# Two attention layers on one core: keys put into class order by ScalarE as they leave PSUM, queries read at a stride of four by the score products

## What is computed

```python
pos = jnp.arange(seq_len)
seg = pos // 64
local = seg[None, :] == seg[:, None]
diff = jnp.abs(pos[None, :] - pos[:, None])
dil = (diff > 0) & (diff % 4 == 0) & (diff <= 4 * 64)
mask = jnp.where(local | dil, 0.0, -jnp.inf)
scores = jnp.einsum('bqhd,bkhd->bhqk', q, k) * scaling + mask
out = jnp.einsum('bhqk,bkhd->bqhd', softmax(scores), v)
```

## Time and profile before

| what | value |
|---|---|
| time, median of three runs | 470.29 us (467.96, 470.29, 470.34) |
| span of the profiled execution | 468.2 us |
| TensorE matmuls busy | 443.3 us, 95% |
| VectorE busy | 394.1 us, 84% |
| ScalarE busy | 333.0 us, 71% |
| GpSimd busy | 296.5 us, 63% |
| granted TensorE clock | 0.998 |

### The profile page before, as it was taken

How to read it: one execution, slowest core, us unless ns; L and a number is a source line. 1 busy time by engine, 2 the same in 40 slices (tenths; PEclk the granted TensorE clock), 3 DMA queues, 4 the chain that set the end, 5 groups by cost and what they waited for, 6 DMA issues and landing times.

```text
span 468.2 us, 17264 instructions
## 1 busy us (share of the span) xinstructions
PE 443.3 (95%) x6440; PEld 348.8 (74%) x6440; DVE 394.1 (84%) x1344; ACT 333.0 (71%) x975; POOL 296.5 (63%) x491
## 2 busy tenths in 40 slices
PE   7999699999999999999999899998987989999996
PEld 5687588888888888888787678887744757558775
DVE  5888598997988899799797697996899989998775
ACT  3678668778768777877786678695566579987533
POOL 4222576687576768667865587665669897674322
PEclk9999999999999999999999999999999999999999
DMA  6477952356345335445455564464000000000003
GB/s 224 175 254 201 276 122 53 75 115 123 75 84 110 74 74 109 81 78 109 86 116 122 110 135 90 77 123 91 1 1 0 0 2 0 2 0 2 1 0 91
DMA packets 136098, 40.53 MB, mean 87 GB/s; under 512 B 104976, under 2 KB 131024, under 8 KB 136016
## 3 DMA queue, kind: packets, MB, share of 16 engines
q1 hardware_dynamic: 135440, 38.38, 35.9%
q10 hardware_dynamic: 576, 1.05, 0.6%
HBM read 29.44 MB, written 9.96 MB: 84 GB/s over the span
## 4 chain that ended last, share of the span: by engine, by line
PE 59%; POOL 9%; DMA 8%; DVE 8%; ACT 7%; SPq 4%; issue 3%; ACTq 0%; POOLq 0%; DVEq 0%
PE psum L464 10%; PE psum L422 10%; PE psum L484 5%; PE psum L1186 5%; PE psum L498 5%; PE psum L495 4%; PE psum L510 4%; PE psum L403 4%; DMA st<-w_rows_dram 3%; DMA w_rows_dram<-st 3%; PE psum L1181 3%; ACT pband L569 3%; PE psum L405 2%; PE psum L404 2%; POOL area L1827 2%
## 5 line engine op out<-in xcount | busy, mean ns | idle before, releaser
L948 POOL TENSOR_SCALAR pband<-pband,fac 128x192 f32<-128x192 f32 x256 | 103.9, 424 | 84.8 <-DVE fac L771 84.7
L569 ACT ACTIVATE pband<-pband,st 128x192 f32<-128x192 f32 x256 | 113.2, 448 | 0.9 <-DVE st L719 0.9
L719 DVE CUSTOM_DVE_ANT_0 pband<-psum,band_mask 128x192 f32<-128x192 f32 x256 | 76.0, 353 | 0.1
L422 PE MATMUL psum<-keys,q_class 64*64 64x192 f32 (+2 forms) x1536 | 66.3, 274 | 0.0
L464 PEld LDWEIGHTS psum<-ident,pband 128*128 128x128 f32 x384 | 45.3, 141 | 25.5 <-issue 17.8
L464 PE MATMUL psum<-ident,pband 128*128 128x128 f32 x384 | 53.1, 273 | 6.1 <-DVE arena L836 3.1
L422 PEld LDWEIGHTS psum<-keys,q_class 64*64 64x64 f32 x1536 | 57.7, 133 | 1.4 <-issue 1.4
L569 ACT ACTIVATION_READ_ACCUMULATOR pband<-pband,st 128x1 f32 x256 | 49.5, 193 | 0.0
L938 POOL COPY q_class<-q_rows 128x512 f32<-128x512 f32 x32 | 36.4, 1137 | 14.0 <-ACT q_rows L609 14.0
L930 POOL COPY keys<-k_rows 128x512 f32<-128x512 f32 x32 | 36.2, 1131 | 14.3 <-issue 7.2
L780 DVE COPY pt<-psum 128x512 f32<-128x512 f32 x64 | 43.6, 682 | 0.4
(11 more groups left out here) (213 smaller groups left out, 1086.4 us busy)
## 6 DMA issues: line engine op xcount, KB each, us to landing
v_rows_dram<-arena SPq DMA_DIRECT2D x32, 256.0 KB, 4.6
v_both<-v_rows_dram SPq DMA_DIRECT2D x32, 256.0 KB, 3.9
v_seg<-v_rows_dram SPq DMA_DIRECT2D x64, 128.0 KB, 3.8
v_side<-v_rows_dram SPq DMA_DIRECT2D x96, 64.0 KB, 2.6
w_rows_dram<-st SPq DMA_DIRECT2D x64, 8.0 KB, 3.0
st<-w_rows_dram SPq DMA_DIRECT2D x64, 8.0 KB, 2.5
arena<-_attn_hidden_states_dram SPq DMA_DIRECT2D x4, 256.0 KB, 3.9
out_dram<-x SPq DMA_DIRECT2D x4, 256.0 KB, 2.5
```

What stands on the lines that cost most here:

```text
L422: return pe.matmul(bank[2 * r + head][rows, at:at + y.shape[1]], x, y, start=True, stop=True, skip_group_check=True)
L569: act.activation(x, x, ACT.Exp, bias=mine[:, head:head + 1], scale=-1.0, accum_out=mine[:, 2 + head:3 + head]).then_inc(s_exp, 1)
L719: dve.tensor_tensor_reduce(pband[:, G % P_SLOTS, c, head, :], bank[2 * r + head][:, at:at + BAND], band_mask[:, (0, 1, 1, 2)[w], SEG * (1 ...
L948: pool.tensor_scalar(x, x, fac[:, F % 2, 1, c, head:head + 1], 1.0, ALU.mult, ALU.mult).then_inc(s_scaled, 1)
```

## The change

ScalarE's `take_keys` writes straight into `keys`: it reads the bank at a stride of four, and writes four runs of 128. `k_rows`, `q_class`, `keys_by_class` and `queries_by_class` are gone, and with them the semaphores `s_kclass` and `s_qclass`. The band products read the stationary queries out of `q_rows` at a stride of four numbers (16 bytes). The segment products stream their 64 keys out of `keys`: sixteen positions by four classes, where the class runs fastest, and a class lies 640 numbers (2560 bytes) from the next. A `zero_pads` function only wraps three lines that were there.

```diff
-        k_rows = sb("k_rows", [P, ROW_SLOTS, WT])
         q_rows = sb("q_rows", [P, ROW_SLOTS, WT])
-        q_class = sb("q_class", [P, ROW_SLOTS, DIL, P])
...
                 if r == 0:
-                    pe.wait_ge(s_qclass, G + 1)
-                    pe.wait_ge(s_kclass, G + 1)
-                    if w < NW - 1:
-                        pe.wait_ge(s_kclass, G + 2)
+                    pe.wait_ge(s_query, G + 1)
+                    pe.wait_ge(s_key, G + (2 if w < NW - 1 else 1))
...
-                    x0, x1 = (q_class[DH * head:DH * (head + 1), G % ROW_SLOTS, c, :] for head in range(2))
+                    x0, x1 = (q_rows[DH * head:DH * (head + 1), G % ROW_SLOTS, :].rearrange("p (x c) -> p c x", c=DIL)[:, c, :]
+                              for head in range(2))
...
                             cols = slice(P * a + SEG * half, P * a + SEG * (half + 1))
+                            first_x = PAD + P * w + CLASS_SEG * (2 * a + half)
                             last = product(head, rows, at, q_rows[dims, G % ROW_SLOTS, cols],
-                                           k_rows[dims, G % ROW_SLOTS, cols])
+                                           keys[dims, p % 2, :, first_x:first_x + CLASS_SEG].rearrange("q c x -> q x c"))
...
                 act.wait_ge(s_proj[1], t + 1)
-                wait(act, s_score, 2 * (t - ROW_SLOTS + 1))
-                wait(act, s_kclass, t - ROW_SLOTS + 1)
-                act.copy(k_rows[:, t % ROW_SLOTS, :], shared_bank[:, :]).then_inc(s_key, 1)
+                p, w = divmod(t, NW)
+                if t == 0:
+                    act.wait_ge(s_const, CONST)
+                wait(act, s_score, 2 * NW * (p - 1))
+                act.copy(keys[:, p % 2, :, PAD + P * w:PAD + P * (w + 1)],
+                         shared_bank[:, :].rearrange("p (x c) -> p c x", c=DIL)).then_inc(s_key, 1)
...
                 wait(act, s_score, 2 * (t - ROW_SLOTS + 1))
-                wait(act, s_qclass, t - ROW_SLOTS + 1)
                 act.copy(q_rows[:, t % ROW_SLOTS, :], shared_bank[:, :]).then_inc(s_query, 1)
...
             for t in range(FIRST_STEP, DRAIN):
                 scale_band(t - 5, 1)
-                keys_by_class(t)
+                
                 scale_seg(t - 5)
                 scale_band(t - 4, 0)
-                queries_by_class(t - 1)
+                
```

More of the change, by code:

```diff
@@ L12 @@
+import math
 from contextlib import ExitStack
@@ L189, in attention @@
     s_proj, s_key, s_query = [sem("s_proj_q"), sem("s_proj_k")], sem("s_key"), sem("s_query")
-    s_kclass, s_qclass = sem("s_kclass"), sem("s_qclass")
     s_score, s_max, s_segmax, s_seg = sem("s_score"), sem("s_max"), sem("s_segmax"), sem("s_seg")
@@ L421, in product @@
                 def product(head, rows, at, x, y):
-                    return pe.matmul(bank[2 * r + head][rows, at:at + y.shape[1]], x, y, start=True, stop=True,
+                    n = math.prod(y.shape[1:])
+                    return pe.matmul(bank[2 * r + head][rows, at:at + n], x, y, start=True, stop=True,
                                      skip_group_check=True)
@@ L836, in take_values, with zero_pads @@
                 dve.tensor_copy(v_slot(i), turn_bank[i % 2][:, :]).then_inc(s_vev[i % 2], 1)
+            def zero_pads():
+                dve.wait_ge(s_wlo, 4)
+                dve.memset(raw[P - R:P, 0:2, 2 * P:FT], 0.0)
+                dve.memset(raw[:, 2, FF:FT], 0.0).then_inc(s_zero, 1)
             def blocks(x):
@@ L883, in _ @@
                 if t == 8:
-                    dve.wait_ge(s_wlo, 4)
-                    dve.memset(raw[P - R:P, 0:2, 2 * P:FT], 0.0)
-                    dve.memset(raw[:, 2, FF:FT], 0.0).then_inc(s_zero, 1)
+                    zero_pads()
                 if QUANT_STEP <= t < QUANT_STEP + 15:
@@ L922, in _ @@
         def _(pool):
[L923 to L939, removed]
             def scale_band(F, r):
@@ L993, in _ @@
             built(pool.tensor_copy(band_mask[:, :, BAND:BAND + SEG], band_mask[:, :, 0:SEG]))
-            keys_by_class(0); keys_by_class(1); queries_by_class(0); keys_by_class(2); queries_by_class(1)
-            keys_by_class(3); queries_by_class(2); keys_by_class(4); queries_by_class(3); scale_band(0, 0)
-            queries_by_class(4); scale_band(0, 1); scale_seg(0); keys_by_class(5); scale_band(1, 0)
+            scale_band(0, 0)
+            scale_band(0, 1); scale_seg(0); scale_band(1, 0)
             for t in range(FIRST_STEP, DRAIN):
                 scale_band(t - 5, 1)
-                keys_by_class(t)
                 scale_seg(t - 5)
                 scale_band(t - 4, 0)
-                queries_by_class(t - 1)
                 if t == 8:
```

## The result

| what | before | after |
|---|---|---|
| time, median of four runs | 469.43 us | 492.40 us |
| ratio | | 1.0484, 95% interval 1.045 to 1.0518 |
| span of the profiled execution | 468.2 us | 490.8 us |
| TensorE matmuls busy | 443.3 us | 473.6 us |
| GpSimd busy | 296.5 us | 226.9 us |

What follows compares the result with a forecast made beforehand. The prediction took TensorE's matmuls to bound the main loop, with GpSimd waiting for others. All terms were 0 us on the 470.3 us median, so 470.3 was likeliest; 8-in-10 range 467.5 to 485.5, the forecast's own 468.5 to 472.3.

Steps and rivals of the forecast that it cites:

- what bounds the kernel: Main loop: set by TensorE's work, busy in every microsecond from 90 to 240 us, while GpSimd waits for others.
- relief of GpSimd: GpSimd's 64 copies, 72.6 us of its time, go; nothing of them is on the path: 0 us.
- GpSimd's wait for `fac`: GpSimd in the loop: freed time becomes longer waiting, from 84.7 us to some 130 to 155 us.
- the copies as a latency: Before the scores: they wait for ScalarE's copy, not GpSimd's second, about 1.1 us less each, but no TensorE wait shows: 0 us.
- ScalarE's copy: Key copy reading PSUM at a stride of four: stays at 0.59 us; upper bound 0.54 us more each, 1.6 us in all.
- the first term: Segment products' strided key reads on TensorE: hidden by the slow f32 column pace, 0 us taken, 14.7 us from above.
- A: Rival, segment products pay for their jumps: half as much again 7.4 us, 477.7 (0.10); doubled 14.7 us, 485.0 (0.12).
- the second and larger term: Band products' strided weight loads: hidden at half of their 14 ns pace, 0 us taken, 21 us from above.
- B: Rival, weight loads lose more than half their pace besides the segments' loss: 14.7 + 21 = 36 us, 506; chance 0.06.
- the row on PSUM: Matmul outputs at a stride of four in PSUM, 0.95 us against 1.06 in one piece: taken as support for hidden strides.

Runs made afterwards that it cites:

- e7: The changed kernel with every stride of the score matmuls taken out, so it computes other scores: 469.34 us against 468.95 for the kernel before, ratio 1.0017.
- e6: Kernel before, with ScalarE writing keys by class, segment keys streamed as runs of 16, VectorE restoring order, `q_class` kept: 467.48 us against 468.95, ratio 0.9976.
- e8: More matmul forms (one quadrant, all 128 rows, f32r, strided output) ahead of the kernel before; f32 at 384 columns: 0.84 ns a column plain, 1.71 at stride 4.
- e1: Kernel before with only the band products' queries read from `q_rows` at a stride of four, GpSimd's query copy gone: 481.05 us against 470.31, ratio 1.0236.
- e3: Kernel before with only ScalarE's key copy writing class order and GpSimd making `k_rows` from `keys`, matmul reads unchanged: 468.67 us, ratio 0.9976.

## Why the prediction was wrong

**Right:** what bounds the kernel. TensorE is always busy in the loop, and relief of GpSimd is worth 0 us: e7 and e6 show it, with GpSimd's wait for `fac` taking up what it lost. I named 130 to 155 us for that wait and it was 203.3. With the loop no longer than before it is 177.4 (e7), since I had left out the 28.3 us that GpSimd stood idle before its copies; the longer loop adds the other 25.9. Right too: the copies as a latency (0 us), and ScalarE's copy at 586 ns; of its upper bound nothing was needed.

**Wrong, the first term:** "the read side can go at twice the pace that an f32 matmul asks for, and a stride that halves that pace would still be hidden". I took the 0.85 ns a column of f32 against the 0.45 of f32r for slack of the reads. e8 shows that it isn't: at a stride of 4 an f32 column takes 1.71 ns, against 0.84 in one piece, and an f32r column 0.92, against 0.46. Each doubles from its own level; what goes on inside was not shown. So A should have been priced at its upper end, 14.7 us. Measured for the segments: 0.44 us for 0.23, 64 x 0.21 = 13.4 us of TensorE's time.

**Wrong, the second and larger term:** the weight loads. The pace of 14 ns in the segments was read rightly, and at a stride of 4 it is 30 ns, as I allowed for. But I set it against the mean of the band, 29 ns a record, and that mean is made of wide and narrow products. With 192 columns the slow load is covered (41 ns with it and without), with 64 it is not (15 and 30). Such a cover has to be taken product by product. The term came out at 0.29 us a call in e1, 18.6 us in all, where I took 0 and had 21 for the upper end. That the upper end is near is luck: it stood on loads of 43 ns, and they measured 30. Nor do the forms explain all of it. Eight records of 64 columns that go from 15 to 30 ns, and eight of 128 that go from an estimated 27 (128 columns over four quadrants at 0.85 ns) to 30, are some 0.14 us of the 0.29. The rest was not traced: no form mixed wide and narrow products as a call does.

**The chances:** B, both losses together, had 0.06 and a time of 506; it is what happened, at 492.4, though not by its condition, since the weight loads lost half their pace and no more. Its TensorE time of 36 us was 30.1, and I had left out that some 7 us of waits would be given back, although I knew these waits. The rule of the Trainium skill that I weighed for A ("SBUF — State Buffer", Specifications (TRN2): lines of 16 bytes, of which an access should hit each twice) agrees with these runs for f32: a stride of 2 numbers is free or nearly so (0.88 against 0.84 ns a column), one of 4 and more costs, runs of 16 are free. For f32r it does not: a stride of 2 hits each line twice as well, and costs 0.88 against 0.46. I discounted it for the row on PSUM, where what the Trainium skill says under "PSUM — Partial Sum Buffer" did not hold and still doesn't (L546); but writes into PSUM were no neighbour of reads from SBUF.

## What to carry to other kernels

Where TensorE bounds the kernel, a copy on an idle engine that lays its operands out in one piece is worth keeping: here 72.6 us of GpSimd's time bought 30.1 us of TensorE's and 23 us of the kernel's. Of the two copies only that of the queries is needed for it: e6 does without that of the keys, at the same time as before. Keep strides of 16 bytes and more out of both operands of f32 matmuls, or make runs of them (and let VectorE or ScalarE put the order right when they read PSUM, which cost 4.1 us of VectorE's time in e6 and none of ScalarE's in e3). Price a cover product by product: a slow weight load hid behind 192 columns and not behind 64; and try the real mix of products, which cost twice what single forms explain.

## What the runs showed of the hardware

- Two strided sides of a matmul cost about what the jumps alone cost (34 ns a record against 33, and 15 plain), not one loss on top of the other.
- f32r pays for a stride of 8 bytes already, 0.88 against 0.46 ns a column, where f32 goes at 0.88 with it and at 1.71 with 16 bytes.
- A strided f32 column took the same time at either level of the granted clock: 1.74 ns in the jumps of e8, in which the clock fell from 1.00 to 0.50 (2.4 to 1.2 GHz) without a change of pace. In one piece a column took 0.84 ns at the full clock and 1.67 at half, so that there a stride of 16 bytes cost 7% (1.78 ns). TensorE had gone over from four quadrants to one before the clock fell, and from one quadrant to all 128 rows before it rose.
- ScalarE reads PSUM at a stride of four at full pace (586 ns for 512 numbers, as in one piece), and f32 matmuls write it so at full pace (15 ns).
